# Context attention in one transformer layer: scores and probabilities with keys on the partitions, sums and division moved

## Chip, cores and metric

One NeuronCore of a Trainium2 chip runs the whole kernel as one program. The metric is the device time in microseconds (us), median of several executions; lower is better.

The engines are named as in the profile: PE (TensorE matrix products; PEld is its loading of the stationary operand), DVE (VectorE), ACT (ScalarE), POOL (GpSimd) and SP, which only issues the loads from memory. Each engine works through its own instructions in order and waits on semaphores for the others. PE writes into eight banks of PSUM; all else lies in SBUF, where a tile is 128 partitions by some elements.

## What is computed

One layer with 256 tokens of width 512: cross attention over a context of 4096 rows, then latent attention with 16 heads, then a mixture of experts. Only the first part is touched:

```python
q = jnp.einsum('bsd,ed->bse', x, wq)
k = jnp.concatenate([k_cache, k_new], axis=1)     # 4096 context rows, then 256 new ones
v = jnp.concatenate([v_cache, v_new], axis=1)
scores = jnp.einsum('bqd,bkd->bqk', q, k) * scale
attn = jax.nn.softmax(scores, axis=-1)
out = jnp.einsum('bqk,bkd->bqd', attn, v)
return jnp.einsum('bqd,ed->bqe', out, wo)
```

There is one head here; x is layer-normalised before this part, and the result is added to the residual.

## The kernel before

All products are made in float32 precision out of three products of a rounded format: every operand is split into a high part (hi, made by ACT with a rounding copy) and the rest (lo, made by DVE as operand minus hi), and a product is hi·hi + hi·lo + lo·hi. In the code that is `product` (L429, L432, L433) and, with the two operands in the other order of parts, `added` (L437 to L439). So each tile that comes from memory costs two halves of `split_hi` on ACT (L277) and two of `split_lo` on DVE (L282: `raw` minus `w_hi`, both in SBUF).

The order of work is written by hand for each engine. The loads go through SP in the order in which the tiles are needed, two tiles ahead; a tile's raw buffer is free when its lo part is made, and its hi and lo buffers when PE has used them (semaphores `used`).

Cross attention goes in these steps:

1. Queries and the new tokens' keys are projected (256-column products), and lie with the feature on the partitions: `q_hi`, `q_lo`, `k_hi`, `k_lo`.
2. **Scores**, `score_group` (L535), 8 groups of 512 context rows and then the 256 new ones: a 128x128 block of queries is stationary, 512 keys move. A group is 2 halves of queries x 4 chunks of features x 3 = 24 products of 512 columns. Scores have queries on the partitions. ACT copies them out of PSUM (L1049); DVE takes the maximum along a row (L1309).
3. The new values are projected (`project_rows`, 24 products of 512 columns).
4. **Value product**, again 8 groups and the new tokens: ACT makes the exponentials with a row's maximum as bias and adds up the row (L1060); PE transposes each 128x128 block of probabilities (`transpose_probs`, L573, 8 per group), since the value product needs keys on the partitions; ACT takes the hi part out of PSUM (`out_hi`, L305) and DVE the lo part (`out_lo`, L309, one operand in PSUM); then `times_values` has the probabilities stationary and 512 columns of context moving, 24 products a group.
5. DVE divides each half of the output by the row sum (L1346), PE transposes it (8 blocks, L455), hi and lo are taken, and the product with wo follows (24 products of 512 columns). DVE adds it to the residual (L1269) and normalises.

POOL has nothing to do between step 1 and step 5. Three of its later instructions (L349 to L354, the rotation of queries in the latent attention) and its first split of latent weights (L282) are used below, because they show how POOL and DVE run beside each other:

```python
def split_lo(eng, t, k, sizes):
    eng.wait_ge(hi_split[k], t.split(k))
    at, n = OFF[k], sizes[k]
    eng.tensor_tensor(w_lo[:, t.slot, at:at + n], raw[:, t.slot, at:at + n],
                      w_hi[:, t.slot, at:at + n].bitcast(F32), ALU.subtract)
```

Of the kernel before, what the change touches and what calls it, by code (L numbers as in the profile page):

```python
# [31 lines left out]
ALU = mybir.AluOpType  # L32
# [43 lines left out]
F01 = dict(ln1=1, s_even=2, s_new=6, pt_even=7, ot=11, ln2=12, rope=13, y=14, ln3=15, h_t=16, moe=16)  # L76
F23 = dict(q=1, s_odd=2, pt_new=6, pt_odd=7, ot=11, qkv=12, rope=13, scores=14, pt=15, ln3=30, moe=30)
# [3 lines left out]
F67 = dict(pv=1, c=2, rows=11)  # L81
# [5 lines left out]
V_LN1, V_Q, V_K, V_V, V_PT, V_OT, V_LN2, V_C, V_M0 = 1, 5, 7, 9, 11, 29, 33, 37, 41  # L87
# [23 lines left out]
def perceiver_layer(nc, x, small, wq, wk, wv, wo, ctx_t, ctx_n, w_qkv, w_rope, w_mla, w_exp, out):  # L111
    with ExitStack() as ctx:
# [20 lines left out]
        neg_max = sb("neg_max", [P, 2])  # L133
        exp_bias = sb("exp_bias", [P, 2])
# [3 lines left out]
        probs = sb("probs", [P, 2, 2, 512])  # L138
        o_row = sb("o_row", [P, 2, D])
# [5 lines left out]
        row_max = sb("row_max", [P, 2, NG + 1])  # L145
        sums = sb("sums", [P, 2, NG + 1])
        row_sum = sb("row_sum", [P, 2])
# [5 lines left out]
        rope_raw = probs[:, :, :, :].rearrange("p a b n -> p (a b) n")  # L153
# [3 lines left out]

        operands = sb("operands", [P, 11776], F32R)
# [10 lines left out]
        k_hi, k_lo = op(2048, NC, T), op(3072, NC, T)  # L169
        v_hi, v_lo = op(4096, 2, D), op(5120, 2, D)  # L170

        pt_hi, pt_lo = op(6144, 2, 2, 512), op(8192, 2, 2, 512)
# [18 lines left out]
        scores = sb("scores", [P, 2, KEYS])  # L191
# [50 lines left out]
        bias_ready = sem("bias_ready")  # L242
        p_ready = sem("p_ready")
        o_ready = sem("o_ready")
# [180 lines left out]
        def _(pe):  # L425
# [9 lines left out]
            def added(o, a, b, start, stop):  # L435

                pe.matmul(o, a[0], b[0], start=start, stop=False, skip_group_check=True)  # L437
                pe.matmul(o, a[0], b[1], start=False, stop=False, skip_group_check=True)  # L438
                return pe.matmul(o, a[1], b[0], start=False, stop=stop, skip_group_check=True)  # L439
# [39 lines left out]
            def project_rows(t, a_hi, a_lo, first_bank, width=512, told=None, split=None, midway=(None, None)):  # L479


                for h in range(2):
                    for c in range(NC):
                        if split is not None and c % 2 == 0:
                            pe.wait_ge(ev_lo, split + 2 * h + c // 2)
                        if h == 0 and c % 2 == 0:
                            ready(t, c // 2)
                        w = wcols(t, OFF[c // 2] + (c % 2) * width, width)
                        ins = product(bank[first_bank + h][:, 0:width],
                                      (a_hi[:, c, half(h)], a_lo[:, c, half(h)]), w, c == 0, c == NC - 1,  # L490
                                      told if h == c == 0 else None)
                        if h == 1 and c == 1:
                            ins.then_inc(used[0], 1)
                        if c == 1 and midway[h] is not None:
                            midway[h]()
                    ins.then_inc(bank_full[first_bank + h], 1)


# [36 lines left out]
            def score_group(j, s):  # L535

                t = Tile(j, T_CT + s)
                for h in range(2):
                    b = 2 * (s % 2) + h
                    if not isinstance(j, int):  # L540
                        pe.wait_ge(s_copied, j * 4 + (2 * s + h - 3))
                    for c in range(NC):
                        if h == 0 and c % 2 == 0:
                            ready(t, c // 2)
                        ins = product(bank[b][:, :], (q_hi[:, c, half(h)], q_lo[:, c, half(h)]),
                                      x_chunk(t, c), c == 0, c == NC - 1,
                                      used[1] if h == c == 0 else None)
                        if h == 1 and c == 1:
                            ins.then_inc(used[0], 1)
                    ins.then_inc(bank_full[b], 1)  # L550
# [6 lines left out]
            for h in range(2):  # L557
                pe.wait_ge(s_copied, 2 * (NG - 2) + h + 1)
                for c in range(NC):
                    ins = product(bank[h][:, 0:T], (q_hi[:, c, half(h)], q_lo[:, c, half(h)]),  # L560
                                  (k_hi[:, c, :], k_lo[:, c, :]), c == 0, c == NC - 1,
                                  used[1] if h == c == 0 else None)
                ins.then_inc(bank_full[h], 1)

            project_rows(Tile(0, T_WV), xt_hi, xt_lo, 4)


            def transpose_probs(ring, exps, blocks=4, told=None):

                for h in range(2):  # L570
                    pe.wait_ge(p_ready, exps + (h + 1))
                    for k in range(blocks):
                        ins = pe.transpose(bank[2 * ring + h][:, k * P:k * P + P],  # L573
                                           probs[:, ring, h, k * P:k * P + P], ident)
                        if told is not None and h == k == 0:
# [1247 lines left out]
```

## Time and profile before

| what | us |
|---|---|
| median of 3 runs (523.3, 525.05, 531.25) | 525.05 |
| the profiled execution, whole | 523.41 |
| its span, first to last instruction | 521.4 |
| PE busy in the span | 510.9 (98%) |
| DVE busy | 389.1 (75%) |
| ACT busy | 304.4 (58%) |
| POOL busy | 29.4 (6%) |

The page of the profile counts an engine as busy while an instruction runs. Matmuls overlap: one of 256 columns is shown 0.28 us long, but the next starts earlier, so the cost of a product is read as the distance between starts. A timeline row merges equal instructions in a row (x8); the bracket at its end is the engine's idle time just before it, and who ended that. In the groups of instructions the last part is busy time, mean length and idle time before.

### The profile page before, as it was taken

How to read it: one execution, taken by the hardware profiler on the slowest of the kernel's cores; microseconds unless marked ns; L12 is line 12 of the kernel's file. 1: busy time of each engine (PE TensorE's matmuls, PEld its weight loads, DVE VectorE, ACT ScalarE, POOL GpSimd, SP SyncE). 2: the span in 40 equal slices, each digit the busy share in tenths (PEclk: the TensorE clock that was granted, in tenths of full speed). 3: DMA queues.
4: the chain of work that ended last, by engine and by line, in shares of the span. 5: the costliest groups of instructions: out<-in, count | busy, mean ns of one | idle time of the engine just before them, and what ended most of it. 6: DMA issues, size and time to landing. Idle time of an engine off the chain costs nothing.

```text
span 521.4 us, 9657 instructions
## 1 busy us (share of the span) xinstructions
PE 510.9 (98%) x3454; PEld 458.6 (88%) x3454; DVE 389.1 (75%) x616; ACT 304.4 (58%) x470; POOL 29.4 (6%) x48
## 2 busy tenths in 40 slices
PE   8999999999999999989999999999999999999997
PEld 7988888888777998969899999999999999999997
DVE  6777555557889888867787777677776877778675
ACT  5665586655367776664664655546565465645631
POOL 1000000000524113001000000000000000000000
PEclk9999999999999999999999999999999999999999
DMA  8775634545412233333545464655656555464521
GB/s 290 295 232 174 198 123 132 167 162 158 152 35 77 77 97 145 121 123 137 203 142 194 171 224 155 224 182 180 210 163 229 163 200 201 165 233 152 215 72 40
DMA packets 19459, 86.24 MB, mean 165 GB/s; under 512 B 2160, under 2 KB 2416, under 8 KB 19312
## 3 DMA queue, kind: packets, MB, share of 16 engines
q1 hardware_dynamic: 19440, 85.99, 49.0%
q8 instruction: 11, 0.18, 0.1%
q14 instruction: 8, 0.07, 0.0%
HBM read 85.46 MB, written 0.52 MB: 165 GB/s over the span
## 4 chain that ended last, share of the span: by engine, by line
PE 90%; DVE 5%; ACT 2%; issue 1%; DMA 1%; SPq 0%; ACTq 0%; DVEq 0%
PE bank L936 31%; PE bank L429 17%; PE bank L433 16%; PE bank L432 16%; PE bank L437 2%; PE bank L438 1%; PE bank L439 1%; PE bank L573 1%; DVE w_lo L282 1%; PE bank L715 1%; DMA raw<-wq_dram 1%; PE bank L735 1%; PE bank L696 1%; ACT operands L305 1%; DVE xt_lo L330 1%
## 5 line engine op out<-in xcount | busy, mean ns | idle before, releaser
L277 ACT CAST w_hi<-raw 128x768 fp32r<-128x768 f32 (+3 forms) x158 | 159.0, 1041 | 96.6 <-PE bank L936 82.6
L282 DVE TENSOR_TENSOR w_lo<-raw,w_hi 128x1280 fp32r<-128x1280 f32 (+3 forms) x156 | 182.8, 1213 | 13.8 <-ACT w_hi L277 11.7
L429 PE MATMUL bank<-w_hi,operands 128*128 128x512 f32 (+1 forms) x322 | 125.8, 391 | 1.6 <-DVE operands L330 1.0
L433 PE MATMUL bank<-w_hi,operands 128*128 128x512 f32 (+1 forms) x322 | 124.5, 387 | 0.0
L432 PE MATMUL bank<-w_lo,operands 128*128 128x512 f32 (+1 forms) x322 | 123.8, 385 | 0.0
L936 PE MATMUL bank<-xt_hi,w_lo 128*128 128x256 f32 x512 | 105.3, 277 | 0.0
L936 PE MATMUL bank<-xt_hi,w_hi 128*128 128x256 f32 x512 | 105.3, 277 | 0.0
L936 PE MATMUL bank<-xt_lo,w_hi 128*128 128x256 f32 x512 | 105.1, 277 | 0.0
L936 PEld LDWEIGHTS bank<-xt_hi,w_hi 128*128 128x128 f32 x512 | 81.8, 188 | 2.6
L936 PEld LDWEIGHTS bank<-xt_lo,w_hi 128*128 128x128 f32 x512 | 79.8, 188 | 0.0
L936 PEld LDWEIGHTS bank<-xt_hi,w_lo 128*128 128x128 f32 x512 | 79.7, 188 | 0.0
L429 PEld LDWEIGHTS bank<-w_hi,operands 128*128 128x128 f32 x322 | 60.5, 188 | 12.5 <-DVE operands L330 1.1
L433 PEld LDWEIGHTS bank<-w_hi,operands 128*128 128x128 f32 x322 | 60.5, 188 | 11.9
L432 PEld LDWEIGHTS bank<-w_lo,operands 128*128 128x128 f32 x322 | 60.6, 188 | 10.5
L1595 DVE SCALAR_TENSOR_TENSOR first_rows<-bank,weights,first_rows 128x512 f32<-128x512 f32 x66 | 49.2, 750 | 18.8 <-PE bank L433 17.8
L309 DVE TENSOR_TENSOR operands<-bank,operands 128x512 fp32r<-128x512 f32 (+1 forms) x73 | 46.3, 674 | 22.6 <-ACT operands L305 22.0
L305 ACT ACTIVATE operands<-bank 128x512 fp32r<-128x512 f32 (+1 forms) x73 | 40.1, 586 | 24.3 <-PE bank L573 13.7
L1607 DVE TENSOR_TENSOR operands<-scores,operands 128x512 fp32r<-128x512 f32 x32 | 22.2, 692 | 39.8 <-ACT operands L1229 39.8
L1223 ACT ACTIVATE scores<-bank 128x512 f32<-128x512 f32 x32 | 19.2, 600 | 32.0 <-PE bank L936 31.9
L1602 DVE TENSOR_TENSOR scores<-bank,scores 128x512 f32<-128x512 f32 x32 | 22.0, 686 | 2.0 <-ACT scores L1223 1.7
L1229 ACT CAST operands<-scores 128x512 fp32r<-128x512 f32 x32 | 19.7, 615 | 1.1 <-DVE scores L1602 1.1
L1309 DVE TENSOR_REDUCE row_max<-scores x16 | 10.8, 682 | 12.0 <-ACT scores L1049 12.0
(182 smaller groups left out, 563.2 us busy)
## 6 DMA issues: line engine op xcount, KB each, us to landing
raw<-w_exp_dram SPq DMA_DIRECT2D x34, 896.0 KB, 4.7
raw<-w_exp_dram SPq DMA_DIRECT2D x34, 640.0 KB, 5.6
raw<-ctx_t_dram SPq DMA_DIRECT2D x16, 512.0 KB, 4.7
raw<-ctx_n_dram SPq DMA_DIRECT2D x16, 512.0 KB, 4.2
raw<-w_mla_dram SPq DMA_DIRECT2D x8, 512.0 KB, 3.5
raw<-w_mla_dram SPq DMA_DIRECT2D x8, 448.0 KB, 3.8
raw<-wq_dram SPq DMA_DIRECT2D x4, 256.0 KB, 5.2
raw<-wk_dram SPq DMA_DIRECT2D x2, 512.0 KB, 7.1
```

What stands on the lines that cost most here:

```text
L277: act.copy(w_hi[:, t.slot, at:at + n], raw[:, t.slot, at:at + n]).then_inc(hi_split[k], 1)
L282: eng.tensor_tensor(w_lo[:, t.slot, at:at + n], raw[:, t.slot, at:at + n], w_hi[:, t.slot, at:at + n].bitcast(F32), ALU.subtract) \
L305: act.activation(hi, bank[b][rows, at:at + n], ACT.Copy, scale=scale).then_inc(ev_hi, 1)
L309: dve.tensor_tensor(lo, bank[b][rows, at:at + n], hi.bitcast(F32), ALU.subtract) \
L429: ins = pe.matmul(o, a[0], b[0], start=start, stop=False)
L432: pe.matmul(o, a[0], b[1], start=False, stop=False)
L433: return pe.matmul(o, a[1], b[0], start=False, stop=stop)
L936: return pe.matmul(bank[b + u][:, m * T:m * T + T], a[:, t.slot, at + m * P:at + m * P + P], x[:, c, :], start=c == 0 and a is w_hi and x ...
L1229: act.copy(h_hi[:, s % 2, :], h_row[:, s % 2, :]).then_inc(ev_hi, 1)
L1595: dve.scalar_tensor_tensor(out=res[:, h, :], in0=bank[b][:, :], scalar=w, in1=res[:, h, :], op0=ALU.mult, op1=ALU.add).then_inc(res_done, 1)
L1602: dve.tensor_tensor(h_row[:, s % 2, :], bank[up][:, :], gate_act[:, s % 2, :], ALU.mult) \
L1607: dve.tensor_tensor(h_lo[:, s % 2, :], h_row[:, s % 2, :], h_hi[:, s % 2, :].bitcast(F32), ALU.subtract).then_inc(ev_lo, 1)
```

## The change

The scores are made the other way round: a 128x128 block of keys is stationary and all 256 queries move, so a group of 512 keys is 4 blocks of keys x 4 chunks x 3 = 48 products of 256 columns, and scores have keys on the partitions. Probabilities are then already in the layout of the value product, which has 128x128 blocks of context stationary and the 256 queries moving (48 products of 256 columns a group, into four banks); its output has features on the partitions, as the product with wo needs it. No probabilities and no outputs are transposed.

The maximum of a query now lies across partitions: DVE keeps an elementwise maximum of all score blocks, PE transposes it, DVE reduces it, PE spreads it to all partitions, and it is subtracted from the scores before the exponential: by DVE for the first two groups, by POOL for the other six. The row sums are added up by POOL over all probability blocks, reduced by DVE and PE, and the division takes place after wo, in the addition to the residual.

```diff
 def score_group(j, s):
-    for h in range(2):
...
-            ins = product(bank[b][:, :], (q_hi[:, c, half(h)], q_lo[:, c, half(h)]),
-                          x_chunk(t, c), c == 0, c == NC - 1,
+    for pair in range(2):
...
+            for k in range(2):
+                ins = added(bank[b][:, k * T:k * T + T], x_chunk(t, c, (2 * pair + k) * P, P),
+                            (q_hi[:, c, :], q_lo[:, c, :]), c == k == 0, c == NC - 1,
...
-def transpose_probs(ring, exps, blocks=4, told=None):
-def times_values(ring, t, number, last=False, midway=None):
+def times_context(j, s):
+    t = Tile(j, T_CN + s)
+    pe.wait_ge(ev_lo, j * 2 + (V_P1 + s - 1))
+    for k in range(4):
+        if k % 2 == 0:
+            ready(t, k // 2)
+        for m in range(NC):
+            ins = product(bank[out_banks[m]][:, 0:T], context_chunk(t, k, m),
+                          (pt_hi[:, s % 2, k, :], pt_lo[:, s % 2, k, :]), False, False)
...
+def transpose_totals():
+    pe.wait_ge(totals, 2)
...
+# ACT
+for g in range(2, NG):
+    t = Tile(0, T_CN + g)
+    v = score_rows[:, g * 1024:g * 1024 + 1024]
+    act.wait_ge(lowered_late, g - 1)
+    exps(v)
+    split_hi(act, t, 0, X_SIZES)
+    act.wait_ge(used[1], t.free(1))
+    probs_hi(g + 4, flat(pt_hi[:, g % 2, :, :]), v)
+    split_hi(act, t, 1, X_SIZES)
...
+# DVE
-dve.tensor_reduce(row_max[:, h, bass.ds(j * 2 + s, 1)],
-                  scores[:, h, bass.ds(j * 1024 + s * 512, 512)], AX, ALU.max)
+dve.tensor_tensor(flat(top_pair), flat(top_pair),
+                  score_rows[:, bass.ds(j * 2048 + (s * 1024 + pair * 512), 512)], ALU.max)
...
+def lower(v, n):
+    dve.tensor_tensor(v, v, bank[1][:, T:2 * T].unsqueeze(1).broadcast_to(both), ALU.subtract)
+def probs_lo(number, hi, lo, v):
+    dve.wait_ge(ev_hi, number)
+    dve.tensor_tensor(lo, v, hi.bitcast(F32), ALU.subtract).then_inc(ev_lo, 1)
...
+def total_rows():
+    dve.wait_ge(summed, NG)
+    dve.tensor_tensor(total_parts[:, 0:2, :], total_parts[:, 0:2, :], total_parts[:, 2:4, :], ALU.add)
...
+def add_attended(h):
+    dve.wait_ge(bank_full[4 + h], F45["wo"])
+    dve.scalar_tensor_tensor(out=res[:, h, :], in0=bank[4 + h][:, :], scalar=row_inv[:, h:h + 1],
+                             in1=res[:, h, :], op0=ALU.mult, op1=ALU.add)
...
+# POOL
+def lower(g):
+    v = by_keys(g * 1024, 4)
+    pool.tensor_tensor(v, v, top_all.unsqueeze(1).broadcast_to([P, 4, T]), ALU.subtract)
+def add_up(g):
+    pool.wait_ge(p_ready, g + 4)
+    pool.wait_ge(summed, g)
+    pool.tensor_tensor(total_parts, total_parts, by_keys(g * 1024, 4), ALU.add).then_inc(summed, 1)
+lower(2)
+lower(3)
...
+for g in range(2, NG - 3):
+    lower(g + 3)
+    add_up(g)
+for g in range(NG - 3, NG):
+    add_up(g)
```

`score_rows`, `tops` and `xn` (which holds `total_parts` here) are tiles in SBUF. The places in SBUF of some operands shift by a few elements, and the raw rotary weights get a buffer of their own.

POOL's instructions between its two square roots of the first norm (L1708 before, L1810 now) and its first split of latent weights. Before there is nothing between them:

```order
L1708 TENSOR_TENSOR rstd<-var_eps,power 128x1 [waits var_ready]
L282 TENSOR_TENSOR w_lo<-raw,w_hi 128x896 [waits hi_split0,lo_split0]
L1708 TENSOR_TENSOR rstd<-var_eps,power 128x1 [waits var_ready] x2
L282 TENSOR_TENSOR w_lo<-raw,w_hi 128x1024 [waits hi_split1,lo_split1]
L363 TENSOR_TENSOR scores<-scores,smalls 128x64 [waits qkv_scaled]
```

Now the same stretch, in which L1822 lowers a group's scores and L1836, L1839 and L1829 add up probabilities:

```order
L1822 TENSOR_TENSOR score_rows<-score_rows,tops 128x1024 [waits s_copied,top_shared]
L1822 TENSOR_TENSOR score_rows<-score_rows,tops 128x1024
L1836 TENSOR_TENSOR xn<-score_rows 128x1024 [waits p_ready]
L1822 TENSOR_TENSOR score_rows<-score_rows,tops 128x1024
L1839 TENSOR_TENSOR xn<-xn,score_rows 128x512 [waits summed]
L1822 TENSOR_TENSOR score_rows<-score_rows,tops 128x1024
L1829 TENSOR_TENSOR xn<-xn,score_rows 128x1024 [waits summed,p_ready]
L1822 TENSOR_TENSOR score_rows<-score_rows,tops 128x1024
L1829 TENSOR_TENSOR xn<-xn,score_rows 128x1024 [waits summed,p_ready]
L1822 TENSOR_TENSOR score_rows<-score_rows,tops 128x1024
L1829 TENSOR_TENSOR xn<-xn,score_rows 128x1024 [waits summed,p_ready] x4
L296 TENSOR_TENSOR w_lo<-raw,w_hi 128x896 [waits hi_split0,lo_split0]
```

Thirteen instructions of 1024 elements and one of 512, all reading and writing SBUF, now stand ahead of POOL's split.

DVE's loop over the context in the value product, one of the two groups of its body. Before, the lo parts of the probabilities are two instructions of 512 elements that read PSUM, followed by the two splits:

```order
L309 TENSOR_TENSOR operands<-bank,operands 128x512 [waits ev_hi]
L308 REGISTER_ALU
L309 TENSOR_TENSOR operands<-bank,operands 128x512 [waits ev_hi]
L280 REGISTER_ALU
L282 TENSOR_TENSOR w_lo<-raw,w_hi 128x1024 [waits hi_split0]
L282 TENSOR_TENSOR w_lo<-raw,w_hi 128x1024 [waits hi_split1]
```

Now the lo part (L1402) is one instruction of 1024 elements that reads the probabilities in SBUF, between the two splits (L296):

```order
L296 TENSOR_TENSOR w_lo<-raw,w_hi 128x1024 [waits hi_split0]
L1401 REGISTER_ALU
L1402 ISA [waits ev_hi]
L1402 TENSOR_TENSOR operands<-score_rows,operands 128x1024
L296 TENSOR_TENSOR w_lo<-raw,w_hi 128x1024 [waits hi_split1]
```

All three of a group's instructions on DVE now have both inputs in SBUF.

## Rows read from the trace of the kernel before

**Rows 1.** The page: PE's busy time; POOL and PE's clock in 40 slices.

```profile
PE 510.9 (98%) x3454; PEld 458.6 (88%) x3454; DVE 389.1 (75%) x616; ACT 304.4 (58%) x470; POOL 29.4 (6%) x48
...
POOL 1000000000524113001000000000000000000000
PEclk9999999999999999999999999999999999999999
```

**Rows 2.** Timeline of PE and ACT around the scores: start, length, engine, line, operation.

```profile
9.38 0.28 PE L433 MATMUL bank<-xt_hi,w_lo 128*128 128x256 f32 x1
...
19.93 0.28 PE L433 MATMUL bank<-xt_hi,w_lo 128*128 128x256 f32 x1
20.04 0.39 PE L429 MATMUL bank<-w_hi,operands 128*128 128x512 f32 x1
...
64.15 0.28 PE L429 MATMUL bank<-operands 128*128 128x256 f32 x1
...
64.44 0.59 ACT L1049 COPY scores<-bank 128x512 f32 x1 [2.16 <-PE bank L433]
...
66.91 0.28 PE L433 MATMUL bank<-operands 128*128 128x256 f32 x1
```

**Rows 3.** Timeline of PE, from the first transposes to the next stage's first product.

```profile
72.63 1.47 PE L573 MATMUL bank<-first_rows,probs 128*128 128x128 f32 x12
74.54 0.50 PE L429 MATMUL bank<-operands 128*128 128x512 f32 x1 [0.43 <-DVE operands L309]
...
77.40 1.04 PE L573 MATMUL bank<-first_rows,probs 128*128 128x128 f32 x8
...
83.77 1.04 PE L573 MATMUL bank<-first_rows,probs 128*128 128x128 f32 x8
...
115.67 1.03 PE L573 MATMUL bank<-first_rows,probs 128*128 128x128 f32 x8
...
133.96 0.66 PE L455 MATMUL bank<-first_rows,xn 128*128 128x128 f32 x4
135.40 0.44 PE L429 MATMUL bank<-w_hi,xt_hi 128*128 128x384 f32 x1 [0.79 <-DVE xt_lo L330]
```

**Rows 4.** Groups of instructions by shape on DVE, ACT, POOL; then a timeline row.

```profile
L282 DVE TENSOR_TENSOR w_lo<-raw,w_hi 128x1024 fp32r<-128x1024 f32 x79 | 95.1, 1221 | 6.6 <-ACT w_hi L277 4.6
...
L309 DVE TENSOR_TENSOR operands<-bank,operands 128x512 fp32r<-128x512 f32 x70 | 45.3, 685 | 21.6 <-ACT operands L305 21.1
...
L277 ACT CAST w_hi<-raw 128x1024 fp32r<-128x1024 f32 x80 | 82.5, 1052 | 88.2 <-PE bank L936 82.6 <-PE bank L433 3.0 <-DMA raw<-ctx_t_dram 1.8
...
L282 POOL TENSOR_TENSOR w_lo<-raw,w_hi 128x1024 fp32r<-128x1024 f32 x1 | 2.4, 2390 | 0.0
...
86.46 2.36 DVE L282 TENSOR_TENSOR w_lo<-raw,w_hi 128x1024 fp32r<-128x1024 f32 x2
```

**Rows 5.** Timeline of POOL and DVE where they run beside each other.

```profile
137.68 2.39 POOL L282 TENSOR_TENSOR w_lo<-raw,w_hi 128x1024 fp32r<-128x1024 f32 x1
137.97 0.76 DVE L330 TENSOR_TENSOR xt_lo<-bank,xt_hi 128x256 fp32r<-128x256 f32 x2 [0.89 <-ACT xt_hi L325]
...
139.68 0.61 DVE L1380 CUSTOM_DVE_ANT_0 scores<-scores 128x192 f32<-128x192 f32 x1
...
142.92 0.35 DVE L1380 CUSTOM_DVE_ANT_0 scores<-scores 128x192 f32<-128x192 f32 x1
...
150.73 0.76 POOL L354 TENSOR_TENSOR scores<-scores 128x256 f32<-128x256 f32 x1
150.93 1.51 DVE L282 TENSOR_TENSOR w_lo<-raw,w_hi 128x896 fp32r<-128x896 f32 x1
...
158.03 1.08 DVE L282 TENSOR_TENSOR w_lo<-raw,w_hi 128x896 fp32r<-128x896 f32 x1
158.17 1.54 POOL L354 TENSOR_TENSOR scores<-scores 128x256 f32<-128x256 f32 x1
...
168.24 0.73 POOL L354 TENSOR_TENSOR scores<-scores 128x256 f32<-128x256 f32 x1
```

More of the change, by code:

```diff
@@ L568, in transpose_probs @@
-            def transpose_probs(ring, exps, blocks=4, told=None):
-                for h in range(2):
[L571 to L575, printed above, removed]
-                            ins.then_inc(told, 1)
-                    ins.then_inc(bank_full[2 * ring + h], 1)
@@ new lines, in project_values @@
+            def project_values():
+                t = Tile(0, T_WV)
+                for h in range(2):
+                    for c in range(NC):
+                        if h == 0 and c % 2 == 0:
+                            ready(t, c // 2)
+                        ins = product(bank[4 + h][:, :], (xt_hi[:, c, half(h)], xt_lo[:, c, half(h)]),
+                                      x_chunk(t, c), c == 0, c == NC - 1)
+                        if h == 1 and c == 1:
+                            ins.then_inc(used[0], 1)
+                        if h == 0 and c == 1:
+                            transpose_tops()
+                    ins.then_inc(bank_full[4 + h], 1)
+                    if h == 0:
+                        share_tops()
@@ L618, in _, with project_out @@
-            project_rows(Tile(0, T_WO), ot_hi, ot_lo, 4, told=used[1], split=V_OT,
-                         midway=(lambda: transpose_half(o_row, 1, 2, o_ready, 2), None))
+                    ins.then_inc(bank_full[out_banks[m]], 1)
+            times_first()
+            times_new()
+            with pe.Fori(0, NG // 2 - 1) as j:
+                times_context(j, 1)
+                times_context(j, 2)
+            times_last()
+            def project_out():
+                t = Tile(0, T_WO)
+                for h in range(2):
+                    for c in range(NC):
+                        if h == 0:
+                            pe.wait_ge(ev_lo, V_OT + c)
+                            if c % 2 == 0:
+                                ready(t, c // 2)
+                        ins = product(bank[4 + h][:, :], (ot_hi[:, c, half(h)], ot_lo[:, c, half(h)]),
+                                      x_chunk(t, c), c == 0, c == NC - 1, used[1] if h == c == 0 else None)
+                        if h == 1 and c == 1:
+                            ins.then_inc(used[0], 1)
+                    ins.then_inc(bank_full[4 + h], 1)
@@ L622, in rest @@
+            project_out()
             def rest(k):
@@ L1063, in probs_hi, with exps @@
-            def probs_hi(ring, full, n=512):
-                for h in range(2):
-                    out_hi(act, 2 * ring + h, full, pt_hi[:, ring, h, 0:n], n)
-            act.wait_ge(bias_ready, 1)
-            exps(1, slice(CTX, KEYS), T, slice(NG, NG + 1))
-            exps(0, slice(0, 512), 512, slice(0, 1))
+            act.wait_ge(s_max, 2 * NG + 2)
+            act.copy(flat(new_keys), bank[0][:, :]).then_inc(s_copied, 1)
+            def exps(v):
+                act.activation(v, v, ACT.Exp, scale=XSCALE).then_inc(p_ready, 1)
```

324 lines of the change are left out of this document (185 added, 139 removed).

## The prediction

> **What bounds the kernel now.** I read the page first: PE is busy 98% of the span, its granted clock is full (2.4 GHz) in every slice, and POOL does nothing from the second to the tenth slice [rows 1]. So time can only be won by giving PE less to do, and lost by making it wait. Second, PE's timeline, for what a product costs. From 9.38 to 19.93 us lie 93 distances between products of 256 columns: 0.113 us each; from 20.04 to 64.15 lie 192 of 512 columns: 0.230 each. Half the columns cost half, so turning the scores round leaves PE's work as it is. The dearest row for 256 columns is the scores of the new tokens, 23 distances from 64.15 to 66.91: 0.120 each [rows 2]. Third, the value product. Transposes start at 83.77 and, five groups later, at 115.67: 6.38 us a group, of which 24 products take 24 x 0.230 = 5.51, so the eight transposes of a group cost 0.87 [rows 3]. Last, where DVE and POOL meet, because POOL gets its first work in this stage.
>
> **The change, part by part: PE alone.** Removed: seven times 0.87 = 6.1; before the first group, 72.63 to 77.40 is 4.77 us, of which 12 products of the new tokens are 2.76, so twelve transposes with a wait of 0.43 were 2.0 [rows 3]; the eight transposes of the output like one group's, 0.9. Sum 9.0. Added: six transposes (maximum, its spreading, row sums), about 1.0 with the switching; waits of 1.3, 0.3 and 0.7, as follows.
>
> The first wait is for the maximum. ACT's last copy of scores ends at 65.0 [rows 2]. Instructions of 512, 1024 and 256 elements on DVE take 0.69, 1.18 to 1.22 and (by the same slope) 0.42 us; a cast on ACT 1.05 [rows 4]. DVE then has the last block's maximum (to 65.9), two splits of the first context tile (to 68.4), the maximum over the new scores and the folding of two blocks: 69.6. PE is through the new scores and the first six value products at 68.3. So it waits 1.3, which nothing hides. Then PE is covered by the rest of the value projection, until about 74.6; DVE's lowering and ACT's exponentials of the first 128 keys, which go in small pieces, are done at about 73.7. The new tokens' lo part is late by 0.3. Behind wo, DVE now takes the output's lo parts and both weight splits ahead of the residual, which makes the wait before the next stage (133.96 to 135.40, [rows 3]) about 0.7 longer. PE alone: -9.0 + 1.0 + 2.3 = -5.7.
>
> ACT's share shrinks a little (one exponential and one copy of 1024 in place of two and two of 512), and the maximum on DVE costs about what the reduction did; both hide under PE's 5.5 a group. The loads are the same.
>
> **POOL beside DVE.** This term decides. POOL gets six lowerings, one first sum, six further sums of 1024 elements, and one of 512. The nearest row is its split of 1024 elements, 2.39 us [rows 4]; four times its 256 elements at 0.73 would be 2.9 [rows 5]. I take 2.39, since the shape is the same; the other end adds 7.7 us if it all counts. A group needs one lowering and one sum, 4.78 us, less than PE's 5.5: if POOL ran undisturbed, it would keep up, and its sums would end near 112, well ahead of their use near 120.
>
> But POOL and DVE do not run undisturbed. The rows of both engines are to be read in pairs [rows 5]. At 137.97 DVE runs two instructions with one operand in PSUM beside POOL's split, and neither is stretched. At 139.68 DVE multiplies a tile in SBUF by itself, two inputs in SBUF, two microseconds into the same POOL instruction: 0.61 us, where the same shape takes 0.35 at 142.92. At 150.93 a split on DVE (two inputs in SBUF) meets a running POOL instruction: 1.51 instead of the 1.08 at 158.03. At 158.17 it is POOL that comes second: 1.54 instead of the 0.73 at 168.24. Each time the second one ends its full length after the first one's end, less 0.13 us: 139.68 + 0.61 = 140.29 is 140.07 + 0.35 - 0.13, 152.44 is 151.49 + 1.08 - 0.13, and 159.71 is 159.11 + 0.73 - 0.13. So an instruction of POOL on SBUF and one of DVE with two inputs in SBUF run one after the other, and each handover gives back 0.13.
>
> Before, this cost nothing in cross attention. Now the lo part of the probabilities, which read PSUM, reads SBUF, and so all three of a group's instructions on DVE are of that kind, as are all of POOL's.
>
> The sum in two ways. *Occupancy*: POOL 13.5 x 2.39 = 32.3; DVE 23 x 1.18 = 27.1 (three for each of seven groups and two for wo, the distance of two splits being 1.18, [rows 4]); 27 handovers give back 3.5. That is 55.9 us which cannot overlap. POOL starts when ACT has copied the spread maxima, behind the first group, the new values and a cast: near 79.8 on this clock. The last of these instructions is then done at 135.7 at best, where without exclusion it would be at 118.3: 17.4 us later. *Turn by turn*, each taking the place after the other: a pair of turns takes 2.39 + 1.18 - 0.26 = 3.31, DVE needs three turns for a group, so a group takes 9.9 us where PE needs 5.5. PE would start groups 1 to 5 near 86.9, 95.7, 105.7, 115.6 and 123.4 (POOL's short instruction makes one step shorter) instead of 83.1, 88.6, 94.0, 99.5 and 105.0, and run freely from there: 18.5 us later at the end. I take 18.5.
>
> The Trainium skill (SBUF — State Buffer, section "Who interferes with whom") says that a DVE instruction with two SBUF inputs contends with a GpSimd instruction that reads SBUF, and that whichever issues first keeps the shared ports for its whole instruction. The rows agree, but for the 0.13; by the page alone, without that saving, the turns would come to 22.2 us and the time to about 539.9.
>
> Sum: 523.4 (the profiled execution) - 5.7 + 18.5 = **536.2 us**. The median of the runs shown is 525.05, 1.6 above that execution, because the three scatter from 523.3 to 531.25; I stay on the execution's footing.
>
> **Rivals.** *No exclusion through a long instruction.* Then PE alone counts: 517.7, not slower. For it: only one of the pairs shows a POOL instruction of 1024 elements, and that one near its end. Against it: all the pairs, to within 0.01 us of each other. It decides if a lowering or sum holds DVE up for 1.2 us or less instead of 2.39 - 0.26 = 2.13, since 13.5 x 0.94 is the 12.7 by which the forecast comes out above the profiled execution. Chance 0.12.
>
> *Dearer narrow products, no exclusion.* At 0.120 in place of 0.115 for some 820 products of 256 columns, 4.1 us come back: 521.8. Only the row with both operands in the same tile shows it [rows 2]. Chance 0.05.
>
> *POOL keeps its turns.* If a waiting DVE instruction does not come between two of POOL's, DVE stands until POOL waits for exponentials, and PE has one long wait, some 22 us, instead of several of 4: the loss is 22, so 539.7. No row shows who is next when both are ready. If PE's clock falls to the lower level behind such a wait, one group at half rate adds 5.5: 545.2. The rows show full clock throughout, but also no wait of that length. The Trainium skill (TensorE: Matmul & The Clock Gate, section "What's actually happening") says that an idle TensorE goes back to 1.2 GHz; no run here shows it so far. Chance 0.13. (The opposite order, DVE first, gives about 537, with PE waiting for the row sums at the end; I count that with the forecast.)
>
> **How the numbers follow.** The forecast, in any order of turns near the one laid out, has 0.70, with its own range from 531 to 542 (saving of 0.13 to 0.25 at a handover, POOL's instruction from 2.3 to 2.6). About 2% is what a measurement of this kernel can tell from no change, some 10.5 us. The forecast lies 11.1 above the median shown and 12.8 above the profiled execution, so of its 0.70 about 0.48 is slower by more than that and 0.22 within. With the third rival: slower 0.61. The first two rivals are within 2%, but for 0.03 of the first, as PE cannot lose more than its 9.0 and a little: same 0.36, faster 0.03. The range leaves out the first two rivals and takes in the rest: 524 to 545.
>
> **What would show it.** Right: in the timeline POOL's L1822 and L1829 and DVE's L296 and L1402 never overlap by more than about 0.13 us; POOL's stretch from 2.4 to about 3.3; PE waits some 4 us before each of the first groups of the value product, its releaser DVE L1402; starts of groups lie near 10 us apart while POOL has work and 5.5 after; scores still take about 44 us. Wrong: POOL's instructions at 2.4 beside busy DVE and no such waits on PE (first rival); score products at 0.12 apart (second); one wait of 20 us (third). If PE waits longer than 1.3 for the maximum, or wo's residual is late by more than 0.7, the small terms are wrong.

## The result, and the profile after

The changed kernel takes 536.0 us (median of 4 runs, 535.09 to 538.18) beside 524.98 for the kernel before on the same chip: a ratio of 1.0177, 95% interval 1.0108 to 1.0245. The forecast was 536.2 us, and 0.61 of its chances lay on slower by over 2%: the ratio lies just short of that border, with its interval on both sides. The profiled execution took 535.09 us, 11.7 more than the one of before; its span of 533.2 is 11.8 longer. The runs of a kernel can fall into two clusters some 5 to 8 us apart (the kernel before, in the second set of experiments: 523.4 to 525.3 and 529.6 to 531.7; the last section shows a difference of this size), so kernels are compared below by ratios and, within the profiles, by the length of the one stage that the change touches.

First the page, to be held against [rows 1]:

```profile
PE 509.7 (96%) x3780; PEld 473.0 (89%) x3780; DVE 420.0 (79%) x614; ACT 301.7 (57%) x438; POOL 73.3 (14%) x62
...
POOL 1000009992154131101000000000000000000000
PEclk9999998989999999999999999999999999999999
```

TensorE has more instructions and yet is busy 1.2 us less, GpSimd is full in the seventh to ninth slice, and the granted clock has two dips just there. VectorE's busy time grew by 31 us with two instructions fewer: its instructions became longer. The groups of the stage (66 to 148 us) show which ones, as [rows 4] did:

```profile
L296 DVE TENSOR_TENSOR w_lo<-raw,w_hi 128x1024 fp32r<-128x1024 f32 x18 | 43.2, 2434 | 1.3 <-ACT w_hi L291 1.2
L1822 POOL TENSOR_TENSOR score_rows<-score_rows,tops 128x1024 f32<-128x1024 f32 x6 | 19.3, 3231 | 72.7 <-ACT tops L1140 72.7
L1829 POOL TENSOR_TENSOR xn<-xn,score_rows 128x1024 f32<-128x1024 f32 x6 | 19.2, 3204 | 5.4 <-ACT score_rows L1122 5.1
L1402 DVE TENSOR_TENSOR operands<-score_rows,operands 128x1024 fp32r<-128x1024 f32 x7 | 16.1, 2294 | 0.0
```

The split on VectorE takes 2.43 us on the mean instead of 1.22, and GpSimd's operations 3.2 instead of the 2.39 of [rows 4]. Next TensorE's timeline from the scores to the next stage, as [rows 2, 3] showed it before: every first product of a group, with the wait ahead of it and its releaser.

```profile
20.09 0.28 PE L451 MATMUL bank<-operands,w_hi 128*128 128x256 f32 x1
...
67.05 0.39 PE L443 MATMUL bank<-w_hi,xt_hi 128*128 128x512 f32 x1
...
69.66 0.44 PE L566 MATMUL bank<-first_rows,tops 128*128 128x128 f32 x2 [1.07 <-DVE tops L1389]
...
86.49 0.39 PE L443 MATMUL bank<-operands,w_hi 128*128 128x256 f32 x1 [3.63 <-DVE operands L1402]
...
95.36 0.38 PE L443 MATMUL bank<-operands,w_hi 128*128 128x256 f32 x1 [1.52 <-DVE operands L1402]
...
105.33 0.58 PE L443 MATMUL bank<-operands,w_hi 128*128 128x256 f32 x1 [3.72 <-DVE operands L1402]
...
115.29 0.58 PE L443 MATMUL bank<-operands,w_hi 128*128 128x256 f32 x1 [2.79 <-DVE operands L1402]
...
123.07 0.38 PE L443 MATMUL bank<-operands,w_hi 128*128 128x256 f32 x1 [0.35 <-DVE operands L1402]
...
145.33 0.60 PE L471 MATMUL bank<-first_rows,xn 128*128 128x128 f32 x4
146.80 0.45 PE L443 MATMUL bank<-w_hi,xt_hi 128*128 128x384 f32 x1 [0.87 <-DVE xt_lo L344]
```

The scores keep their length: 20.09 to the first product of the value projection at 67.05 is 46.96 us. The next stage begins at 146.80 where it began at 135.40 [rows 3]: 11.4 of the 11.8 us of span are lost between those two points. What is left, 0.4, lies in the rest of the program and was not followed up. Five waits on VectorE's lo part of the probabilities (L1402) add up to 12.0 us, with full steps of 10 us from group to group (95.36 to 105.33 to 115.29) where there were 6.38. Last the two engines that wait for each other, answering to [rows 5]:

```profile
82.98 3.37 DVE L1402 TENSOR_TENSOR operands<-score_rows,operands 128x1024 fp32r<-128x1024 f32 x1
85.23 3.38 POOL L1836 TENSOR_TENSOR xn<-score_rows 128x1024 f32<-128x1024 f32 x1
86.28 6.73 DVE L296 TENSOR_TENSOR w_lo<-raw,w_hi 128x1024 fp32r<-128x1024 f32 x2
88.56 3.36 POOL L1822 TENSOR_TENSOR score_rows<-score_rows,tops 128x1024 f32<-128x1024 f32 x1
91.89 2.26 POOL L1839 TENSOR_TENSOR xn<-xn,score_rows 128x512 f32<-128x512 f32 x1
92.93 2.30 DVE L1402 TENSOR_TENSOR operands<-score_rows,operands 128x1024 fp32r<-128x1024 f32 x1
```

A row's length here holds the time in which the instruction stood. VectorE's L1402 ends at 86.35. GpSimd's sum, on record since 85.23, ends at 88.61: 2.26 us after that, which is its own 2.39 less 0.13. VectorE's next, on record since 86.28, comes only then. So the turns alternate, one each, and a pair of them takes 3.33 us (88.56 to 91.89).

### The profile page after: what moved, and what is told of

It is laid out like the page before. It is cut to its first block, busy times and chain, and to the rows that moved or that the text cites. A ratio compares the mean times of both kernels' runs of the same rounds, so it can differ in the third digit from the quotient of the medians.

```text
span 533.2 us, 10271 instructions
## 1 busy us (share of the span) xinstructions
PE 509.7 (96%) x3780; PEld 473.0 (89%) x3780; DVE 420.0 (79%) x614; ACT 301.7 (57%) x438; POOL 73.3 (14%) x62
## 4 chain that ended last, share of the span: by engine, by line
PE 71%; DVE 16%; DMA 4%; issue 4%; ACT 4%; SPq 0%; POOL 0%; DVEq 0%; ACTq 0%
PE bank L1001 31%; PE bank L443 10%; PE bank L447 9%; PE bank L446 9%; DVE w_lo L296 7%; PE bank L451 3%; PE bank L455 3%; PE bank L454 3%; DMA raw<-w_mla_dram 3%; ACT w_hi L291 1%; DVE operands L1402 1%; DMA raw<-ctx_t_dram 1%; DVE score_rows L1538 1%; ACT score_rows L1122 1%; DVE xt_lo L344 1%
## 5 line engine op out<-in xcount | busy, mean ns | idle before, releaser
L296 DVE TENSOR_TENSOR w_lo<-raw,w_hi 128x1280 fp32r<-128x1280 f32 (+3 forms) x156 | 204.5, 1353 | 14.0 <-ACT w_hi L291 12.8
L1001 PE MATMUL bank<-xt_hi,w_lo 128*128 128x256 f32 x512 | 105.3, 277 | 0.0
L1001 PE MATMUL bank<-xt_hi,w_hi 128*128 128x256 f32 x512 | 105.3, 277 | 0.0
L1001 PE MATMUL bank<-xt_lo,w_hi 128*128 128x256 f32 x512 | 105.1, 277 | 0.0
L1001 PEld LDWEIGHTS bank<-xt_hi,w_hi 128*128 128x128 f32 x512 | 81.8, 188 | 2.7
L1001 PEld LDWEIGHTS bank<-xt_lo,w_hi 128*128 128x128 f32 x512 | 79.7, 188 | 0.0
L1001 PEld LDWEIGHTS bank<-xt_hi,w_lo 128*128 128x128 f32 x512 | 79.7, 188 | 0.0
L443 PE MATMUL bank<-w_hi,operands 128*128 128x512 f32 (+1 forms) x194 | 75.1, 387 | 1.6 <-DVE operands L344 1.0
L447 PE MATMUL bank<-w_hi,operands 128*128 128x512 f32 (+1 forms) x194 | 74.1, 382 | 0.0
L446 PE MATMUL bank<-w_lo,operands 128*128 128x512 f32 (+1 forms) x194 | 73.8, 380 | 0.0
L1709 DVE TENSOR_TENSOR operands<-score_rows,operands 128x512 fp32r<-128x512 f32 x32 | 22.2, 693 | 40.6 <-ACT operands L1297 40.6
L443 PE MATMUL bank<-operands,w_hi 128*128 128x256 f32 x128 | 38.5, 301 | 12.2 <-DVE operands L1402 12.0
L451 PE MATMUL bank<-operands,w_hi 128*128 128x256 f32 x160 | 45.1, 282 | 1.0 <-DVE operands L344 0.6
L454 PE MATMUL bank<-operands,w_hi 128*128 128x256 f32 x160 | 44.2, 276 | 0.0
L455 PE MATMUL bank<-operands,w_lo 128*128 128x256 f32 x160 | 44.2, 276 | 0.0
L443 PEld LDWEIGHTS bank<-w_hi,operands 128*128 128x128 f32 x194 | 36.5, 188 | 7.5 <-DVE operands L344 1.1
L447 PEld LDWEIGHTS bank<-w_hi,operands 128*128 128x128 f32 x194 | 36.4, 188 | 6.8
L446 PEld LDWEIGHTS bank<-w_lo,operands 128*128 128x128 f32 x194 | 36.5, 188 | 5.4
L319 ACT ACTIVATE operands<-bank 128x512 fp32r<-128x512 f32 (+1 forms) x59 | 32.3, 577 | 13.4 <-PE bank L447 7.1
L323 DVE TENSOR_TENSOR operands<-bank,operands 128x512 fp32r<-128x512 f32 (+1 forms) x59 | 36.7, 662 | 2.7 <-ACT operands L319 2.2
```

Of the source, the lines that this page charges most:

```text
L319: act.activation(hi, bank[b][rows, at:at + n], ACT.Copy, scale=scale).then_inc(ev_hi, 1)
L323: dve.tensor_tensor(lo, bank[b][rows, at:at + n], hi.bitcast(F32), ALU.subtract) \
L443: ins = pe.matmul(o, a[0], b[0], start=start, stop=False)
L446: pe.matmul(o, a[0], b[1], start=False, stop=False)
L447: return pe.matmul(o, a[1], b[0], start=False, stop=stop)
L451: ins = pe.matmul(o, a[0], b[0], start=start, stop=False, skip_group_check=True)
```

## The experiments

Two theories were put to the test. The first is the forecast's: an instruction of GpSimd on SBUF and one of VectorE with two inputs in SBUF run one after the other, so that TensorE waits for VectorE. The other is that the loss lies in the amount of work: too much for VectorE, too much for GpSimd (lowerings or sums), or too much for TensorE with its narrow products. The measure that is freest of everything else is the length of the stage from the first product of the value projection to the first product of the next stage (in the kernel before 67.03 to 135.40). It stands here for all profiles together, with the rest of the span behind the stage:

| kernel | stage, us | beside the changed kernel | behind it, us | profiled execution, us |
|---|---|---|---|---|
| before | 68.37 | -11.38 | 386.0 | 523.41 |
| changed | 79.75 | - | 386.4 | 535.09 |
| three VectorE operations read PSUM | 61.10; again 62.61 | -18.65; -17.14 | 386.1; again 391.9 | 518.30; again 523.30 |
| lo part alone reads PSUM | 70.39 | -9.36 | 385.8 | 527.14 |
| six sums left out | 75.36; again 74.27 | -4.39; -5.48 | 392.9; again 392.9 | 539.00; again 537.65 |
| GpSimd idle, its work on VectorE | 65.01 | -14.74 | 385.8 | 520.82 |
| common maximum, sums on GpSimd | 65.37 | -14.38 | 385.8 | 520.39 |
| common maximum, sums on VectorE | 59.39 | -20.36 | 385.9 | 514.24 |

### VectorE reads one operand from PSUM

Nothing of GpSimd's work is touched and nobody gets less to do. Of VectorE's three operations of a group, and of its two for the output projection's weights, the second input is taken from the bank that holds the spread maxima (256 columns, read four times over), so the numbers that come out are others.

```diff
+            def other(v):
+                return v.rearrange("p (k t) -> p k t", t=T), bank[1][:, T:2 * T].unsqueeze(1).broadcast_to([P, 4, T])
...
-                    split_lo(dve, t, 0, X_SIZES)
-                    probs_lo(j * 2 + (V_P1 + s - 1), ...)
-                    split_lo(dve, t, 1, X_SIZES)
+                    split_lo_psum(t, 0)
+                    probs_lo_psum(j * 2 + (V_P1 + s - 1), ...)
+                    split_lo_psum(t, 1)
```

> The changed kernel with one thing different: in the value product, DVE's three instructions of a group (two splits, the probabilities' lo part) and the two splits for wo take their second operand from PSUM instead of SBUF. Same count, same length, same POOL work; what they subtract is not the hi part, so the lo parts are not the reference's. Theory (an instruction of POOL on SBUF and one of DVE with two SBUF inputs run one after the other): POOL's L1822 and L1829 fall from 3.3 to 2.4 us, no wait of PE over 1.5 us is left in the value product, groups start 5.5 apart, time 535.1 - 18.5 = about 516.6. Rival 1 (POOL's subtraction and sums are slow by themselves, 3.3 us): POOL keeps 3.3, PE waits only at the end for the row sums, about 521. Rival 2 (the ring of two probability buffers between PE, ACT and DVE sets the pace): nothing changes, about 535.

Measured 518.3 us. The timeline of both engines:

```profile
81.52 4.96 POOL L1838 TENSOR_TENSOR score_rows<-score_rows,tops 128x1024 f32<-128x1024 f32 x2 [74.81 <-ACT tops L1140]
83.53 1.22 DVE L1410 TENSOR_TENSOR operands<-score_rows,bank 128x1024 fp32r<-128x1024 f32 x1 [0.57 <-ACT operands L1126]
84.67 1.22 DVE L1416 TENSOR_TENSOR w_lo<-raw,bank 128x1024 fp32r<-128x1024 f32 x1
...
86.43 2.42 POOL L1852 TENSOR_TENSOR xn<-score_rows 128x1024 f32<-128x1024 f32 x1
```

Side by side, VectorE takes 1.22 us and GpSimd 2.42, and from 82 us on to the end of the value product TensorE waits for nobody. The same shapes, counts and queues, with one operand elsewhere, and the stage is 18.65 us shorter. The work of the engines is therefore not what costs, nor the two buffers for probabilities, which are the same here. The same kernel again, with more executions:

> VectorE's two splits, its lo part and its split of the output projection's weights read one operand from a bank instead of from SBUF (so the numbers are others), once more and timed against the kernel before. Exclusion between operations with two SBUF operands each predicts what the first look gave, about 517 us with a ratio to the kernel before of 0.985, all of the 18.5 us gone. If the first look was a chance, over 530.

522.6 us by the median, ratio to the kernel before 0.984 (0.976 to 0.992), stage 62.61: the gain holds, as 17.1 us here. In this run the products of the value product stood 0.118 apart, in the first one mostly 0.113 (more on that at the end).

### Only the lo part reads PSUM

```diff
                     split_lo(dve, t, 0, X_SIZES)
-                    probs_lo(j * 2 + (V_P1 + s - 1), ...)
+                    probs_lo_psum(j * 2 + (V_P1 + s - 1), ...)
                     split_lo(dve, t, 1, X_SIZES)
```

> As the run before, but only the probabilities' lo part takes its second operand from PSUM; the splits of the context stay as they are. One of three contending instructions of DVE in a group is then free. Theory, turn by turn: DVE needs two turns of 3.3 us for a group while POOL has work, so groups start some 6.6 apart instead of 10; the loss of 18.5 shrinks by about 9: 526. Rival 1 (POOL slow by itself): no change against the run with all three in PSUM. Rival 2 (ring of two buffers): 535.

Measured 527.14 us, stage 9.36 shorter: the middle value between both. Two of a group's three VectorE operations still take turns with GpSimd, and TensorE's groups go by their pace:

```profile
105.19 0.38 PE L443 MATMUL bank<-operands,w_hi 128*128 128x256 f32 x1 [0.78 <-DVE operands L1410]
...
111.87 0.38 PE L443 MATMUL bank<-operands,w_hi 128*128 128x256 f32 x1 [0.95 <-DVE operands L1410]
...
118.53 0.38 PE L443 MATMUL bank<-operands,w_hi 128*128 128x256 f32 x1 [0.75 <-DVE operands L1410]
```

6.68 and 6.66 us apart: two turns of 3.33. (One earlier step, from 92.95 to 98.50, is 5.55; GpSimd's short sum lies in it.) With three turns it is 10, with none TensorE's own 5.5. The granted clock was 1.00 throughout this run, so these waits cost by themselves, without a lower clock. The price goes with the number of turns, not with the number of instructions.

### The six sums left out

```diff
-                dve.wait_ge(summed, NG)
+                dve.wait_ge(summed, 2)
...
             for g in range(2, NG - 3):
                 lower(g + 3)
-                add_up(g)
-            for g in range(NG - 3, NG):
-                add_up(g)
+            pool.wait_ge(summed, 2)
```

> The changed kernel without POOL's six sums over the groups 2 to 7 (the row sums are then those of the first two groups and the new tokens alone, so the division is not the reference's). POOL keeps its six lowerings, the first sum and the short one. Theory: the turns of 3.3 us last as long as POOL has work, 8.5 x 3.3 = 27 us from 79.4, so groups 1 and 2 start near 87 and 97 and the others 5.5 to 6 apart: the loss of 18.5 shrinks by about 10, time near 525. Rival 1 (POOL slow by itself): POOL is far ahead then, near 517. Rival 2 (ring of two buffers): 535.

A miss: 539.0 us. Two things are in it. Behind the stage the rest of the program took 392.9 us instead of 386, though nothing was changed there. And the stage itself became only 4.4 shorter, not 10. It was run again:

> The six sums of GpSimd left out, its lowerings kept, once more and timed. The look before ran its 256-column products of the expert stage 0.118 us apart instead of 0.113 at the same granted clock, some 6.5 us that nothing in the edit touches, and gave 539.0. Without that I expect about 531: TensorE ends this stage some 4 us before the changed kernel's, not 10 as I had first worked out, since groups 2 and 3 still wait 3.6 us each behind a lowering and TensorE then runs at the lower clock with no wait to hide it. The theory that only the count of GpSimd's operations matters keeps 525; the theory that the sums cost nothing gives 536.

532.65 us by the median, ratio to the kernel before 1.007 (1.002 to 1.013); stage 5.48 shorter. TensorE's and GpSimd's rows of this second run:

```profile
80.93 5.86 POOL L1822 TENSOR_TENSOR score_rows<-score_rows,tops 128x1024 f32<-128x1024 f32 x2 [74.12 <-ACT tops L1140]
...
88.01 0.38 PE L443 MATMUL bank<-operands,w_hi 128*128 128x256 f32 x1 [3.63 <-DVE operands L1402]
...
95.63 10.00 POOL L1822 TENSOR_TENSOR score_rows<-score_rows,tops 128x1024 f32<-128x1024 f32 x3
...
96.89 0.57 PE L443 MATMUL bank<-operands,w_hi 128*128 128x256 f32 x1 [2.62 <-DVE operands L1402]
...
106.86 0.58 PE L443 MATMUL bank<-operands,w_hi 128*128 128x256 f32 x1 [2.88 <-DVE operands L1402]
```

Counted from the value projection (68.69 in this run), groups 1 to 3 start after 19.32, 28.20 and 38.17 us; in the changed kernel, from 67.05, after 19.44, 28.31 and 38.28. To within 0.12 nothing is gained there. With the sums gone the lowerings, which wait for nothing, move up and take the turns that the sums leave free; only when the last of them ends, at 105.63, is VectorE alone. GpSimd's stretch, 24.7 us from 80.93 on, was not what the expectation had wrong: it said 27 (with one turn too many, 8.5 for 7.5). But it let only groups 1 and 2 go by turns, and the three turns of group 3 lie in this stretch too. Behind the wait of 2.88 the clock was at its lower level besides, and no later wait took that up. What counts is not how many instructions GpSimd has, but how long it always has one ready while TensorE waits for VectorE.

### GpSimd given nothing

```diff
...
+            for g in range(2, NG):
+                t = Tile(0, T_CN + g)
+                split_lo(dve, t, 0, X_SIZES)
+                probs_lo(V_P1 + g - 1, ...)
+                if g + 1 < NG:
+                    lower(by_keys(g * 1024 + 1024, 4), 4)
+                split_lo(dve, t, 1, X_SIZES)
+                dve.wait_ge(p_ready, g + 4)
+                dve.wait_ge(summed, g)
+                dve.tensor_tensor(total_parts, total_parts, by_keys(g * 1024, 4), ALU.add).then_inc(summed, 1)
```

> GpSimd is given nothing in this stage: the lowerings of groups 2 to 7 and all sums stand in VectorE's own order, with the same reads and writes. If GpSimd and VectorE go one after the other at these operands, VectorE's twenty-odd extra operations cost it about 1.2 us each instead of GpSimd's 2.3 and the lock is gone: VectorE's operations at 1.2 us everywhere, groups 5.9 to 6.0 us apart (five VectorE operations a group) instead of 9.9, few and short waits of TensorE, no fall of its clock, 522 us. The theory that VectorE simply has too much work after the change gives the opposite: with six sums and six lowerings more on VectorE, later groups and over 540 us. The theory that the clock's fall carries the loss gives about 526.

525.89 us by the median, ratio 0.993 (0.988 to 0.998); the profiled execution 520.82. VectorE now has five operations a group, in a row:

```profile
91.36 1.22 DVE L296 TENSOR_TENSOR w_lo<-raw,w_hi 128x1024 fp32r<-128x1024 f32 x1
92.49 1.22 DVE L1437 TENSOR_TENSOR xn<-xn,score_rows 128x1024 f32<-128x1024 f32 x1
93.63 1.22 DVE L296 TENSOR_TENSOR w_lo<-raw,w_hi 128x1024 fp32r<-128x1024 f32 x1
94.77 1.22 DVE L1402 TENSOR_TENSOR operands<-score_rows,operands 128x1024 fp32r<-128x1024 f32 x1
95.90 1.21 DVE L1397 TENSOR_TENSOR score_rows<-score_rows,bank 128x1024 f32<-128x1024 f32 x1
97.03 1.21 DVE L296 TENSOR_TENSOR w_lo<-raw,w_hi 128x1024 fp32r<-128x1024 f32 x1
```

From 91.36 to 97.03 a group takes 5.67 us, 0.2 more than TensorE's. Of all runs this speaks most plainly against "too much work for VectorE": given the whole of GpSimd's work it is done with a group in 5.67 us, and with GpSimd's help in 10. All of GpSimd's fourteen operations moved to the engine that takes 1.2 us for one instead of 2.39, and the stage became 14.7 us shorter. The third theory of the expectation, that the fall of the clock carries the loss, had put the time at 526 us. The median of 525.89 does not bear it out, since the kernel before had 529.82 here by its median; the profiled execution's 520.82 speaks against it, and so does the stage, since the lower clock lengthens the changed kernel's products by 4.8 us in all (worked out below), not by 14.7.

### One common maximum instead of the lowering

The products are turned round as in the change, but one maximum over all queries and keys goes to ScalarE as the exponential's bias, so no lowering is needed. It asks that no query's largest score lies so far below the common one that its exponentials vanish. Once the sums stay on GpSimd, once they are VectorE's.

```diff
-                act.activation(v, v, ACT.Exp, scale=XSCALE).then_inc(p_ready, 1)
+                act.activation(v, v, ACT.Exp, bias=top_row[:, 1:2], scale=XSCALE).then_inc(p_ready, 1)
...
-            for g in range(2, NG - 3):
-                lower(g + 3)
+            for g in range(2, NG):
                 add_up(g)
```

> One common maximum as ScalarE's bias, so no lowering at all (its rounding differs a little, the quotient is the same), but the sums stay on GpSimd. A group then holds one GpSimd operation of 2.13 us beside three VectorE ones of 1.2: one after the other 5.7 us, against 5.5 us of TensorE. Exclusion predicts VectorE operations stretched to 3.3 us wherever a sum waits beside them, one wait of TensorE of some 3 us early (group 2) and little after, 519 us. No exclusion would give what the kernel with idle GpSimd gave, 514 us; if the lowering were not the cost but the sums, 530 us.

523.61 us by the median, ratio 0.988 (0.977 to 0.999); profiled 520.39. As expected, GpSimd's sums still stretch what they meet, and TensorE has one wait of 3 us, at group 2, behind which the clock falls for 15 products:

```profile
87.65 3.38 DVE L1380 TENSOR_TENSOR operands<-score_rows,operands 128x1024 fp32r<-128x1024 f32 x1
...
91.16 0.38 PE L443 MATMUL bank<-operands,w_hi 128*128 128x256 f32 x1 [2.96 <-DVE operands L1380]
...
107.11 2.87 POOL L1794 TENSOR_TENSOR xn<-xn,score_rows 128x1024 f32<-128x1024 f32 x1 [2.74 <-ACT score_rows L1110]
108.01 3.05 DVE L296 TENSOR_TENSOR w_lo<-raw,w_hi 128x1024 fp32r<-128x1024 f32 x1 [0.28 <-ACT w_hi L291]
```

Later the sum comes beside one split only, and the group keeps TensorE's 5.5 us: there the exclusion costs nothing, since VectorE has room for it. With the sums on VectorE too:

```diff
+                dve.wait_ge(summed, g)
+                dve.tensor_tensor(total_parts, total_parts, by_keys(g * 1024, 4), ALU.add).then_inc(summed, 1)
```

> The changed kernel without any lowering of scores: one maximum over all queries and keys (a softmax is the same for any shift) is given to ACT's exponential as its bias, and the row sums are added up by DVE, so POOL has no work in cross attention. DVE per group: two splits, the lo part, one sum, 4 x 1.18 = 4.7 us, under PE's 5.5. Only one transpose is left for the maximum, and it lies behind half of the value projection. Theory: groups start 5.5 apart, no wait over 0.5 us in the value product, and the gain on PE of about 8 us is kept: 515. Rival 2 (ring of two buffers): 535 less the shorter start, 533. If DVE, now busier, is the bound: some 6 us more, 521.

518.09 us by the median, profiled 514.24, ratio 0.985 (0.978 to 0.991): 1.5% faster than the kernel before, clear of no change though short of 2%, and faster than the changed one. There is no wait in the value product, and the stage is 9.0 us shorter than before the change. That is what the turned products are worth when nothing of GpSimd stands beside VectorE and no lowering is asked for.

## Why the prediction was right

**PE alone, -5.7.** The stage with the exclusion taken out is 61.10 or 62.61 us, so TensorE alone gives -7.3 or -5.8 against the 68.37 of before; the term was right, or up to 1.6 too small. Its three waits were read too long. For the maximum TensorE stood 1.07 us instead of 1.3; for the new tokens' lo part not at all instead of 0.3; and from the transposes at 145.33 to the next product at 146.80 it is 1.47 us, as before (1.44 in [rows 3]), not 0.7 more, because the output's lo parts and the weight splits were done by then. That is 1.2 of the 1.4 us by which the stage came out ahead of the forecast (11.4 against 12.8). That 536.2 lies 0.2 from the median is partly luck: the forecast stands on the profiled execution, and there the time is 535.09, 1.1 less. The score products stand 0.113 apart in this trace, so the rival with dearer narrow products fails in the profiled execution; in four others they stood 0.118 apart (last section).

**POOL beside DVE, +18.5.** Taking the exclusion away shortens the stage by 18.65 us, in the second run by 17.1. The working by turns holds step by step:

| start of group | 1 | 2 | 3 | 4 | 5 |
|---|---|---|---|---|---|
| forecast, us | 86.9 | 95.7 | 105.7 | 115.6 | 123.4 |
| measured, us | 86.49 | 95.36 | 105.33 | 115.29 | 123.07 |

All five are early by 0.3 to 0.4, most of the 0.5 by which the first two waits ahead of them came out short. A pair of turns takes 3.33 us (forecast 3.31), a handover gives back 0.13, the order alternates, GpSimd's short sum makes one step shorter. Both ends named for GpSimd's own duration can now be told apart: 2.39 to 2.42 us beside a VectorE that reads PSUM, so the nearest row had been the right one, not the 2.9. (Two side figures of the prediction come out smaller from its own rows: 2.9 for 2.39 us adds some 7 us, not 7.7, and 27 handovers without the saving bring 18.5 to 22.0, not 22.2. Nothing hung on them.) The Trainium skill (SBUF — State Buffer, section "Who interferes with whom") adds that a VectorE instruction with at most one SBUF input, outside its two-port modes, does not contend with GpSimd. This case agrees: 1.22 and 2.42 us side by side in the first experiment.

**The rivals.** No exclusion would have left GpSimd at 2.4 us beside busy VectorE with no waits of TensorE; the trace has 3.37 and 12.0 us of waits. GpSimd did not keep its turns, so there is no single long wait. But one clause of that rival came true without its condition: the clock did fall, behind waits of 2.8 to 3.7 us. Why that cost no more is next.

**What was not foreseen: the clock.** The stage in windows of 10 us (busy time of PE, PEld, DVE, ACT and POOL, then granted clock, DMA share and GB/s):

```profile
85.00:95.00 10.00, 7.34 (x48) 7.15 (x48) 10.00 (x4) 4.23 (x6) 10.00 (x5) 0.83 0.36 109
95.00:105.00 10.00, 6.08 (x48) 5.68 (x48) 10.00 (x4) 5.83 (x6) 10.00 (x4) 1.00 0.43 138
105.00:115.00 10.00, 7.16 (x48) 6.97 (x48) 10.00 (x4) 3.52 (x4) 9.86 (x4) 0.83 0.33 108
115.00:125.00 10.00, 9.37 (x64) 9.18 (x65) 10.00 (x6) 3.77 (x5) 5.58 (x2) 0.83 0.33 102
```

In the first two windows VectorE and GpSimd are both recorded as full for 10 of 10 us, which they are only in turns. TensorE's clock is at the lower of its two levels, 1.2 GHz, for part of three windows, and its products are then 0.21 apart instead of 0.115. Some 16 of them a time cost 1.6 us more, three times: 4.8 us. They hardly show in the result, because VectorE alone sets when the next group starts: slow products only use up what would have been the next wait (1.52 us at 95.36, where the turns alone would have left 3.4 by estimate, the step of 8.87 less TensorE's 5.5). So the sum held although the share of waits in it was smaller than thought.

## What to carry to other kernels

Before work is given to GpSimd in order to relieve VectorE, look where both would read: if GpSimd reads SBUF and VectorE has two inputs there, their times add up, and a GpSimd operation that is "off the path" costs its whole length as soon as VectorE is what TensorE waits for. Three ways out showed here, all faster than the change: one VectorE operand read from PSUM (the lo part's alone took back 9.4 us in its one execution; a form of it that keeps the computation was not built), the work done by VectorE itself in half the time, or the operation folded into ScalarE's bias. And a nearest row for a contention is to be read in pairs, as starts and ends of both engines; a mean of a group shows a stretched instruction, but not who held it.

## What the runs showed of the hardware that was not expected

**TensorE's clock falls inside a stage.** The timeline of the changed kernel's TensorE behind the wait of 3.63 us that ended at 86.49:

```profile
87.75 0.28 PE L446 MATMUL bank<-operands,w_hi 128*128 128x256 f32 x1
87.86 0.31 PE L447 MATMUL bank<-operands,w_lo 128*128 128x256 f32 x1
87.97 0.41 PE L443 MATMUL bank<-operands,w_hi 128*128 128x256 f32 x1
88.18 0.42 PE L446 MATMUL bank<-operands,w_hi 128*128 128x256 f32 x1
...
91.38 0.29 PE L446 MATMUL bank<-operands,w_hi 128*128 128x256 f32 x1
```

It starts at full pace (0.115 apart), falls to 0.213 at 87.97 and is back at 91.4. Behind the waits of 3.72 and 2.79 us the first product is already slow (0.58 us long in the rows above), as behind those of 2.62 and 2.88 in the experiment without sums; behind the wait of 1.52 and the waits of 0.7 to 1.5 in the one with the lo part in PSUM, nothing fell. The length of the wait does not decide it alone: behind the wait of 3.63 us that ended at 88.01 in the second run without sums the products kept full pace, and the granted clock from 88 to 92 us was 1.00. What decides it stays open. The Trainium skill (TensorE: Matmul & The Clock Gate, section "What's actually happening") has an idle TensorE go back to 1.2 GHz. Most of these rows agree, and they show that it also catches an engine that is busy for most of the stage (7.34 of 10 us in the window from 85 us on).

**Products of 256 columns have two distances at the same full clock.** TensorE's timeline in the expert stage, first of the second run without sums, then of the changed kernel:

```profile
302.92 0.40 PE L1001 MATMUL bank<-xt_hi,w_hi 128*128 128x256 f32 x2
303.16 0.40 PE L1001 MATMUL bank<-xt_hi,w_lo 128*128 128x256 f32 x2
303.39 0.40 PE L1001 MATMUL bank<-xt_lo,w_hi 128*128 128x256 f32 x2
```

```profile
300.13 0.39 PE L1001 MATMUL bank<-xt_lo,w_hi 128*128 128x256 f32 x2
300.36 0.39 PE L1001 MATMUL bank<-xt_hi,w_hi 128*128 128x256 f32 x2
300.59 0.39 PE L1001 MATMUL bank<-xt_hi,w_lo 128*128 128x256 f32 x2
```

Two products in 0.237 us there, 0.227 here, the granted clock 1.00 in both; those of 512 columns keep their 0.23. Over the whole expert stage this comes to two lengths: from the first product of L1001 (L936 before, L989 with the common maximum) to the last it is 267.35 us in three of the ten profiled executions and 261.15 to 261.18 in the other seven. These 6.2 us are nearly all of the difference of 392.9 to 386 us behind the stage, and in the scores the wider distance made some runs start the value projection 2 us later (69.28 instead of 67.05). Which of the two a run gets does not go with the edit: the same kernel showed both. What decides it stays open. A change of 2% is therefore better judged by the length of its stage than by one time, and a stage only where the difference is more than the 2 us that the two distances can make in it (an estimate: some 400 products, 0.005 us each).
